# Preparing a head's queries and keys: one GpSimd sum over 128 partitions, rounding on ScalarE, placement by DMA

## The chip, the cores and the metric

The kernel runs on one core of a Trainium2 chip. The metric is the device time of one execution in microseconds, the median of several runs. A core has five engines that run side by side, each with its own stream of instructions in order: TensorE (PE in the profile; PEld are its weight loads), VectorE (DVE), ScalarE (ACT), GpSimd (POOL) and SyncE (SP), which here issues DMAs. They tell each other through semaphores that something is done. SBUF is the memory of 128 partitions from which the engines work; TensorE writes to PSUM.

## The reference

Two decoder layers over 2048 tokens of width 256. The change touches only the second layer's attention, a latent attention with 16 heads:

```python
kv_c = _linear(x, d_kv_w, d_kv_b)               # 2048 x 64
q_c_lat = _linear(x, d_q_w, d_q_b)              # 2048 x 64
q_c = _linear(q_c_lat, u_q_w, u_q_b)            # 16 heads x 128
k_c = _linear(kv_c, u_k_w, u_k_b)
q_r = _rope(_linear(q_c_lat, qr_w, qr_b))       # 16 heads x 64, rotated by position
k_r = _rope(_linear(kv_c, qr_w, qr_b))
scores = einsum('bqhd,bkhd->bhqk', concat(q_c, q_r), concat(k_c, k_r)) * scale
probs = softmax(scores)                         # no mask
ctx = einsum('bhqk,bkhd->bqhd', probs, v)
return _linear(ctx, out_w, out_b)
```

`_rope` makes `x1*cos - x2*sin` and `x1*sin + x2*cos` of every pair of rows.

## The kernel before, in words

The second attention (function `second_attention`) runs over 16 heads x 16 tiles of 128 queries; a tile's number is `n`, its place in the head is 0 to 15 ("tile 12" below is a place). The 2048 keys of a tile are two halves `g` of 1024. float32 precision comes from pairs: a value is rounded to `hi` (type F32R), and `lo` is the rest; products use lo*hi + hi*lo + hi*hi.

For every tile:

- TensorE makes the scores of each half into PSUM (L1078 to L1080, six products), the context of the tile two before (L1094, L1095, 32 products), in half of the time an output product (L1110, five), and one of the next head's preparation products into `psP` (`project`, L1055 to L1062). In its stream the order for a tile is: scores(n + 1, 0), both context halves of n - 2, the output, `project`, scores(n + 1, 1).
- VectorE takes each half's minimum (L1159) and makes the shift (L1167); `low` (L1175) makes the second float16 part of the probabilities, `prob - parts`; both inputs lie in SBUF. In between: `rden` (L1185), and for the next head `rotate` (L1143) or `rest` (L1149).
- ScalarE takes the exponential of each half (L1224), rounds it to float16 (`high`, L1234), takes the context out of PSUM (`both_sums`, L1243), in the next head's preparation `fold` (L1214), and takes outputs (`part`, L1251). `low` needs `high`.
- SP issues a DMA transpose of each half's two float16 parts (L1349), 128 x 2048 x 2 bytes, after `low`; the context products need it landed. In every second head it also transposes a batch of four contexts of half that size (L1359), once in four tiles.
- GpSimd splits contexts (`split`: L1307, L1309, L1311), adds outputs to `x2` (`add`, L1318), and prepares the next head.

Outputs are taken nine tiles late, so they fall on tiles 9 to 15 of the odd heads and 0 to 8 of the even ones behind them.

The next head is prepared in four chunks of 512 tokens, each of three pieces: two products that VectorE multiplies by cosine and sine into `rot[0]` and `rot[1]` (tiles 3j and 3j + 1 for chunk j), and a third whose results `fold` and `rest` take (tile 3j + 2). The sum `rot[0] + rot[1]` has the rotated queries in rows 64 to 127 (`rotary`) and the rotated keys in rows 0 to 63 (`latent`). The queries belong in rows 64 to 127 of `q_hi` and `q_lo`, the keys in rows 64 to 127 of `k_hi` and `k_lo`. Before, GpSimd does it in six instructions of 64 rows x 512, called `join`: the sum rounded into place (`hi`), the same sum unrounded (`whole`), and `whole - hi` (`lo`), first for the queries and then for the keys. Two steps stand in each of the tiles 2 to 13, one ahead of `add` and one behind the wait for `low(n, 0)`, ahead of `split`. After tile 13 `take_weights` copies a head's weights in eight small casts (L1274) and one copy (L1277).

For head 0 the same steps run ahead of the first scores, one after another.

## Time and profile before

| | us |
|---|---|
| median of 3 runs | 2907.39 |
| lowest, highest | 2907.08, 2911.09 |
| the profiled execution | 2912.68 |
| its span, first to last instruction | 2911.4 |
| mean granted TensorE clock in it | 0.921 |

Busy time of the engines over the span: TensorE 2305.6 us (79%), VectorE 2364.0 (81%), ScalarE 1820.9 (63%), GpSimd 1454.5 (50%). A busy share is a mean over stages with different limits, so the rows further down are cut by stage: a row of windows gives the busy time of each engine in a stretch, the granted clock of TensorE (1.00 is 2.4 GHz, 0.50 is 1.2 GHz), the busy share of the DMA engines and the rate. A row of the timeline has the start, the length, the engine, the line, the operation, output <- inputs with their shapes, and in brackets the idle time in front of the instruction and who ended it. The second attention's heads run from 1134 us to 2692 us of the span.

### The profile page before, as it was taken

The page shows a single profiled execution, that of the slowest core. Times are in us where ns is not written, and L with a number is a line of the kernel's source. Part 1 is how long each engine was busy: PE and PEld are TensorE (multiplying, and loading weights), DVE is VectorE, ACT ScalarE, POOL GpSimd, SP SyncE. Part 2 cuts the span into 40 slices and gives each one's busy share as a digit, 9 for nine tenths or more (in the row PEclk, how much of TensorE's full clock was granted, in tenths as well). Part 3 has the DMA queues.
Part 4 walks back from the last instruction along what each step waited for, and adds up shares of the span by engine and source line. Part 5 has one row for each costly group of instructions (what it writes and reads, how often), then busy time and mean ns, then how long its engine had stood idle before and what let it go on. Part 6 is the DMA issues. An engine that isn't in the chain of part 4 may idle for free. (4 is left out here: it accounts for less than half of the span.)

```text
span 2911.4 us, 50632 instructions
## 1 busy us (share of the span) xinstructions
PE 2305.6 (79%) x18576; PEld 1581.4 (54%) x18576; DVE 2364.0 (81%) x3182; ACT 1820.9 (63%) x2455; POOL 1454.5 (50%) x1640
## 2 busy tenths in 40 slices
PE   3688888765665246899888988988888889888699
PEld 1244454422222124667666666776666667666387
DVE  4688888678888465999999999999999999998422
ACT  2677777534333204878777878877777778777211
POOL 2412121036665206677668577676775686752300
PEclk8799999877787567999999999999999999999799
DMA  3000000000000404999999999999999999999200
GB/s 109 1 1 2 1 2 1 1 1 1 1 0 1 98 0 68 184 182 176 181 173 170 189 179 172 186 173 180 175 171 182 175 173 187 175 174 190 68 15 15
DMA packets 1117159, 300.68 MB, mean 103 GB/s; under 512 B 1107121, under 2 KB 1114257, under 8 KB 1116049
## 3 DMA queue, kind: packets, MB, share of 16 engines
q1 hardware_dynamic: 1115104, 295.74, 57.0%
q8 instruction: 149, 2.44, 0.3%
q10 hardware_dynamic: 1808, 1.71, 0.2%
q14 instruction: 98, 0.79, 0.1%
HBM read 18.45 MB, written 2.10 MB: 7 GB/s over the span
## 5 line engine op out<-in xcount | busy, mean ns | idle before, releaser
L1175 DVE TENSOR_TENSOR parts<-prob,parts 128x1024 f16<-128x1024 f32 x512 | 721.0, 1408 | 22.8 <-ACT parts L1234 20.9
L1224 ACT ACTIVATE prob<-psS,shift 128x1024 f32<-128x1024 f32 x512 | 569.7, 1113 | 237.7 <-DVE shift L1167 236.9
L1159 DVE TENSOR_REDUCE lows<-psS 128x1 f32<-128x1024 f32 x512 | 621.0, 1213 | 43.4 <-PE psS L1080 41.3
L1234 ACT CAST parts<-prob 128x1024 f16<-128x1024 f32 x512 | 535.7, 1046 | 15.8
L1094 PE MATMUL psOb<-kv,partsT 128*128 128x130 f16 x4096 | 418.0, 223 | 157.4 <-ACT part L1251 68.5
L1094 PEld LDWEIGHTS psOb<-kv,partsT 128*128 128x128 f16 x4096 | 363.9, 98 | 262.3 <-issue 176.5
L1078 PE MATMUL psS<-k_hi,q_lo 128*128 128x512 f32 x1024 | 432.5, 422 | 37.7 <-ACT prob L1224 29.6
L1095 PE MATMUL psOb<-kv,partsT 128*128 128x66 f16 x4096 | 406.0, 194 | 0.0
L1080 PE MATMUL psS<-k_hi,q_hi 128*128 128x512 f32 x1024 | 404.2, 395 | 0.0
L1079 PE MATMUL psS<-k_lo,q_hi 128*128 128x512 f32 x1024 | 403.8, 394 | 0.0
L1095 PEld LDWEIGHTS psOb<-kv,partsT 128*128 128x128 f16 x4096 | 365.3, 98 | 0.0
L502 ACT ACTIVATE PT<-psS 128x1024 bf16<-128x1024 f32 (+1 forms) x320 | 280.2, 899 | 65.5 <-PE psS L358 40.5
L1078 PEld LDWEIGHTS psS<-k_hi,q_lo 128*128 128x128 f32 x1024 | 194.8, 190 | 147.5 <-ACT prob L1224 90.5
L1307 POOL TENSOR_TENSOR both_sums<-both_sums 128x64 f32<-128x64 f32 x256 | 154.9, 605 | 219.9 <-DVE parts L1175 195.2
L419 DVE TENSOR_REDUCE pm<-psT 128x1 f32<-128x512 f32 (+3 forms) x320 | 207.0, 647 | 51.6 <-PE psT L329 40.2
L751 POOL TENSOR_TENSOR sel<-Lg,two 128x2048 bf16<-128x2048 f32 x32 | 145.2, 4537 | 194.6 <-DVE gap L657 193.3
L550 POOL TENSOR_TENSOR qB<-nmT,blocks 32x512 bf16<-32x512 bf16 x64 | 73.9, 1155 | 306.7 <-DVE qB L435 303.9
L1080 PEld LDWEIGHTS psS<-k_hi,q_hi 128*128 128x128 f32 x1024 | 194.1, 190 | 45.1
L718 ACT ACTIVATE sel<-sel 128x512 bf16<-128x512 bf16 x128 | 78.6, 615 | 214.6 <-DVE sel L664 214.6
L1079 PEld LDWEIGHTS psS<-k_lo,q_hi 128*128 128x128 f32 x1024 | 195.1, 191 | 32.4
L419 DVE TENSOR_REDUCE pm<-psU 128x1 f32<-128x512 f32 (+3 forms) x320 | 181.2, 566 | 22.9 <-PE psU L332 11.1
L355 PE MATMUL psS<-qB,kT 128*128 128x512 bf16 (+3 forms) x640 | 177.8, 349 | 20.5 <-ACT b L479 16.9
(254 smaller groups left out, 4340.6 us busy)
## 6 DMA issues: line engine op xcount, KB each, us to landing
partsT<-parts SPq DMA_TRANSPOSE x512, 4.5
rf<-in_rwT SPq DMA_DIRECT2D x1, 2048.0 KB, 12.1
ef<-in_ewT SPq DMA_DIRECT2D x1, 2048.0 KB, 17.6
trig<-in_trig SPq DMA_DIRECT2D x2, 1024.0 KB, 10.0
outw_s<-in_outwT SPq DMA_DIRECT2D x1, 2048.0 KB, 17.5
out_x<-ot SPq DMA_DIRECT2D x16, 128.0 KB, 1.7
wug<-in_wupT SPq DMA_DIRECT2D x1, 1024.0 KB, 5.5
wug<-in_wgateT SPq DMA_DIRECT2D x1, 1024.0 KB, 7.6
```

The source lines that it names most:

```text
L355: ins = pe.matmul(bank, kT[:, pair % 2, m * P:(m + 1) * P], qB[:, h, c * BANK + r * P:(c + 1) * BANK], start=True, stop=not diag)
L419: dve.tensor_reduce(pm[:, h, r, j:j + 1], psT[n["max"] % 2][:, 0:w], AX_X, ALU.max).then_inc(max_taken, 1)
L502: act.activation(PT[:, h, first:first + width], psS[:, x * BANK:x * BANK + width], ACT.Exp).then_inc(exp_done, 1)
L1078: pe.matmul(bank, q_lo[:, slot, q], k_hi[b][:, k], start=True, stop=False)
L1079: pe.matmul(bank, q_hi[:, slot, q], k_lo[b][:, k], start=False, stop=False)
L1080: ins = pe.matmul(bank, q_hi[:, slot, q], k_hi[b][:, k], start=False, stop=True)
L1094: pe.matmul(psO[:, 0:KW], partsT[:, s, 0, m, :], kv16[:, block, :], start=(block == 0), stop=False)
L1095: ins = pe.matmul(psO[:, 0:REST], partsT[:, s, 1, m, :], kv16[:, block, 0:REST], start=False, stop=(block == NT - 1))
L1159: dve.tensor_reduce(lows[:, n % 2, g:g + 1], psS[:, (2 * n + g) % 3, :], AX_X, ALU.min).then_inc(half_min, 1)
L1175: dve.tensor_tensor(parts[:, s, 1, :], prob[:, g, :], parts[:, s, 0, :], ALU.subtract).then_inc(low_done, 1)
L1224: act.activation(prob[:, g, :], psS[:, (2 * n + g) % 3, :], ACT.Exp, bias=shift[:, n % 2:n % 2 + 1], scale=-1.0).then_inc(exp_done, 1)
L1234: act.copy(parts[:, s, 0, :], prob[:, g, :]).then_inc(high_done, 1)
```

## The change

The six `join` steps of a chunk are replaced. GpSimd makes one sum over all 128 rows into `whole` (`add_up`). ScalarE rounds it into a new tile `rounded` (`round_sums`), between `exponential(n, 1)` and `high(n, 1)`, in tiles 3, 6, 9 and 12. SP copies the two halves of `rounded` into `q_hi` and `k_hi` by two DMAs (`move_sums`), between the transposes of the same tiles. GpSimd makes the two rests (`rest_queries`, `rest_keys`). All three GpSimd steps stand behind the wait for `low(n, 0)`, one a tile in tiles 2 to 13. `rot` has one buffer instead of two. `take_weights` moves from the end of tile 13 to tile 14, behind that tile's `add`. GpSimd's wait for `low_done` 2n now stands in every tile. The first scores of a head wait for rests and moves instead of `joined`.

```diff
-        rot = [sb(L, f"rot{r}", [P, 2, BANK]) for r in range(2)]
-        whole = sb(L, "whole", [C, BANK])
+        rot = [sb(L, f"rot{r}", [P, BANK]) for r in range(2)]
+        whole = sb(L, "whole", [P, BANK])
+        rounded = sb(L, "rounded", [P, BANK], F32R)
...
-                    pe.wait_ge(joined, 24 * (head + 1))
+                    pe.wait_ge(rests_done, 8 * (head + 1))
+                    pe.wait_ge(moved, 128 * (head + 1))
...
-                if 4 * head + j >= 2:
-                    dve.wait_ge(joined, 24 * head + 6 * (j - 1))
+                if 4 * head + j:
+                    dve.wait_ge(added_up, 4 * head + j)
...
+            def round_sums(head, j):
+                c = 4 * head + j
+                act.wait_ge(added_up, c + 1)
+                if c:
+                    act.wait_ge(rests_done, 2 * c)
+                    act.wait_ge(moved, 32 * c)
+                act.copy(rounded[:, :], whole[:, :]).then_inc(round_done, 1)
...
                 exponential(n, 1)
                 if n < TILES and piece_at(n) is not None and piece_at(n) % 3 == 2:
                     fold(n // NT + 1, piece_at(n), 2 * (n + 1))
+                if n < TILES and n // NT + 1 < NH and n % NT in (3, 6, 9, 12):
+                    round_sums(n // NT + 1, n % NT // 3 - 1)
                 high(n, 1)
...
+            def add_up(head, j):
+                c = 4 * head + j
+                pool.wait_ge(rotated, 2 * c + 2)
+                if c:
+                    pool.wait_ge(rests_done, 2 * c)
+                pool.tensor_tensor(whole[:, :], rot[0][:, :], rot[1][:, :], ALU.add).then_inc(added_up, 1)
+                pool.wait_ge(added_up, c + 1)
+
+            def rest_queries(head, j, halves_scored):
+                slot = q_slot(head, j)
+                pool.wait_ge(round_done, 4 * head + j + 1)
+                if halves_scored:
+                    pool.wait_ge(score_ready, halves_scored)
+                pool.tensor_tensor(q_lo[rotary, slot, :], whole[rotary, :], rounded[rotary, :].bitcast(F32),
+                                   ALU.subtract).then_inc(rests_done, 1)
+                pool.wait_ge(rests_done, 8 * head + 2 * j + 1)
...
-                joins = n < TILES and head < NH and 2 <= i <= 13
-                if joins:
+                ahead = n < TILES and head < NH
+                if n < TILES:
                     pool.wait_ge(low_done, 2 * n)
-                    join(head, j, 2 * turn, n)
                 add(n - LATER - 1)
+                if ahead and i == 14 and head + 1 < NH:
+                    take_weights(head + 1)
                 if n < TILES:
                     pool.wait_ge(low_done, 2 * n + 1)
-                if joins:
-                    join(head, j, 2 * turn + 1, n)
+                if ahead and 2 <= i <= 13 and turn == 0:
+                    add_up(head, j)
+                if ahead and 2 <= i <= 13 and turn == 1:
+                    rest_queries(head, j, 2 * (n + 1))
+                if ahead and 2 <= i <= 13 and turn == 2:
+                    rest_keys(head, j)
                 split(n - 3)
-                if n < TILES and i == 13 and head + 1 < NH:
-                    take_weights(head + 1)
...
+            def move_sums(head, j, halves_scored):
+                sp.wait_ge(round_done, 4 * head + j + 1)
+                if halves_scored:
+                    sp.wait_ge(score_ready, halves_scored)
+                sp.dma_start(q_hi[rotary, q_slot(head, j), :].bitcast(F32), rounded[rotary, :].bitcast(F32)).then_inc(moved, 16)
+                sp.dma_start(k_hi[head % 2][rotary, j * BANK:(j + 1) * BANK].bitcast(F32),
+                             rounded[latent, :].bitcast(F32)).then_inc(moved, 16)
...
                     turn_probabilities(n, 0)
+                if n < TILES and n // NT + 1 < NH and n % NT in (3, 6, 9, 12):
+                    move_sums(n // NT + 1, n % NT // 3 - 1, 2 * (n + 1))
                 turn_contexts(n - 4)
```

## Rows read from the trace of the kernel before

**Rows 1.** The page: busy time, share, instructions; and the group of reductions.

```profile
PE 2305.6 (79%) x18576; PEld 1581.4 (54%) x18576; DVE 2364.0 (81%) x3182; ACT 1820.9 (63%) x2455; POOL 1454.5 (50%) x1640
...
L1159 DVE TENSOR_REDUCE lows<-psS 128x1 f32<-128x1024 f32 x512 | 621.0, 1213 | 43.4 <-PE psS L1080 41.3
```

**Rows 2.** Windows by head, `low` (L1175) alone: heads 0, 12, 15, sum.

```profile
1134.30:1226.30 92.00, 42.80 (x32) 1.00 1.01 175
...
2308.30:2405.10 96.80, 46.79 (x33) 1.00 1.02 176
...
2600.90:2692.40 91.50, 39.21 (x32) 0.94 1.11 186
sum 1558.10, DVE 720.97; mean DVE 45.06
```

**Rows 3.** Windows, all engines: heads 1, 12, 13, 15; PE, PEld, DVE, ACT, POOL.

```profile
1226.30:1323.60 97.30, 87.75 (x788) 68.78 (x786) 93.46 (x110) 77.95 (x92) 66.29 (x88) 0.98 1.06 183
...
2308.30:2405.10 96.80, 85.86 (x780) 65.88 (x778) 94.92 (x110) 78.54 (x94) 73.20 (x90) 1.00 1.02 176
2405.10:2503.80 98.70, 87.95 (x787) 68.53 (x784) 92.70 (x109) 77.37 (x92) 65.52 (x88) 0.98 1.04 181
...
2600.90:2692.40 91.50, 74.90 (x708) 59.33 (x705) 76.10 (x92) 71.79 (x85) 21.74 (x55) 0.94 1.11 186
```

**Rows 4.** Timeline of GpSimd and VectorE, one tile of head 12; VectorE in head 13.

```profile
2351.71 1.29 POOL L1291 TENSOR_TENSOR whole<-rot 64x512 f32<-64x512 f32 x1
2353.08 1.60 POOL L1318 TENSOR_TENSOR x<-x,part 128x256 f32<-128x256 f32 x1
...
2351.89 2.20 DVE L1175 TENSOR_TENSOR parts<-prob,parts 128x1024 f16<-128x1024 f32 x1
...
2486.35 1.65 DVE L1175 TENSOR_TENSOR parts<-prob,parts 128x1024 f16<-128x1024 f32 x1
```

**Rows 5.** Timeline at head 13's end: GpSimd, ScalarE, VectorE; windows of the stretch behind.

```profile
2488.93 1.43 POOL L1274 CAST wr_hi<-qr_hi 64x64 fp32r<-64x64 f32 x2
...
2493.57 0.72 POOL L1318 TENSOR_TENSOR x<-x,part 128x256 f32<-128x256 f32 x1
...
2494.38 0.37 ACT L1251 COPY part<-psOb 128x256 f32<-128x256 f32 x1 [3.35 <-POOL x L1318]
...
2496.88 1.23 DVE L1175 TENSOR_TENSOR parts<-prob,parts 128x1024 f16<-128x1024 f32 x1 [2.90 <-ACT parts L1234]
...
2495.00:2498.40 3.40, 3.40 (x38) 3.13 (x36) 1.23 (x1) 3.34 (x4) 1.20 (x3) 0.50 0.63 117
```

**Rows 6.** DMA issues, KB each, median us to landing; windows in the last head.

```profile
partsT<-parts SPq DMA_TRANSPOSE x512, 4.5
rf<-in_rwT SPq DMA_DIRECT2D x1, 2048.0 KB, 12.1
...
out_x<-ot SPq DMA_DIRECT2D x16, 128.0 KB, 1.7
...
2632.00:2648.00 16.00, 14.24 (x136) 11.15 (x136) 15.53 (x19) 13.76 (x17) 2.86 (x10) 1.00 1.17 203
```

**Rows 7.** Groups of ScalarE with shapes: busy us, mean ns, idle before.

```profile
L1224 ACT ACTIVATE prob<-psS,shift 128x1024 f32<-128x1024 f32 x512 | 569.7, 1113 | 237.7 <-DVE shift L1167 236.9
L1234 ACT CAST parts<-prob 128x1024 f16<-128x1024 f32 x512 | 535.7, 1046 | 15.8
...
L1243 ACT ACTIVATE both_sums<-psOb,rden 128x128 f32<-128x128 f32 x256 | 93.7, 366 | 55.4 <-DVE rden L1185 53.7
L718 ACT ACTIVATE sel<-sel 128x512 bf16<-128x512 bf16 x128 | 78.6, 615 | 214.6 <-DVE sel L664 214.6
```

**Rows 8.** Timeline of TensorE in head 13: context products behind a landing, next scores.

```profile
2468.15 0.23 PE L1094 MATMUL psOb<-kv,partsT 128*128 128x130 f16 x1 [0.37 <-DMA partsT<-parts]
...
2470.38 0.50 PE L1078 MATMUL psS<-k_hi,q_lo 128*128 128x512 f32 x1
```

**Rows 9.** Timeline of GpSimd: the last `join` in front of head 0.

```profile
1124.31 1.25 POOL L1294 TENSOR_TENSOR k_lo<-whole,k_hi 64x512 fp32r<-64x512 f32 x1
```

More of the change, by code:

```diff
@@ L1140, in rotate @@
                 dve.wait_ge(piece_ready, 12 * head + piece + 1)
-                if 4 * head + j >= 2:
-                    dve.wait_ge(joined, 24 * head + 6 * (j - 1))
-                dve.scalar_tensor_tensor(out=rot[kind][:, j % 2, :], in0=psP[:, :], scalar=br[kind][:, head:head + 1],
+                if 4 * head + j:
+                    dve.wait_ge(added_up, 4 * head + j)
+                dve.scalar_tensor_tensor(out=rot[kind][:, :], in0=psP[:, :], scalar=br[kind][:, head:head + 1],
                                          in1=trig[:, kind, cols], op0=ALU.add, op1=ALU.mult).then_inc(rotated, 1)
@@ L1254, in scalar @@
                 fold(0, piece, 0)
+                round_sums(0, piece // 3)
             for n in range(TILES + LATER):
@@ L1278, in take_weights, with rest_keys @@
                 pool.wait_ge(weights_in, done + 1)
-            def join(head, j, step, n):
-                cols, b, slot = slice(j * BANK, (j + 1) * BANK), head % 2, q_slot(head, j)
-                done = 24 * head + 6 * j + step
-                if head:
-                    pool.wait_ge(score_ready, 2 * (n + 1))
-                if step == 0:
-                    pool.wait_ge(rotated, 8 * head + 2 * j + 2)
-                rows, hi, lo = ((rotary, q_hi[rotary, slot, :], q_lo[rotary, slot, :]),
-                                (latent, k_hi[b][rotary, cols], k_lo[b][rotary, cols]))[step // 3]
-                if step % 3 < 2:
-                    pool.tensor_tensor((hi, whole[:, :])[step % 3], rot[0][rows, j % 2, :], rot[1][rows, j % 2, :],
-                                       ALU.add).then_inc(joined, 1)
-                else:
-                    pool.tensor_tensor(lo, whole[:, :], hi.bitcast(F32), ALU.subtract).then_inc(joined, 1)
-                pool.wait_ge(joined, done + 1)
+            def add_up(head, j):
[13 more added lines that the diff above has]
+                pool.wait_ge(rests_done, 8 * head + 2 * j + 1)
+            def rest_keys(head, j):
+                pool.wait_ge(round_done, 4 * head + j + 1)
+                pool.tensor_tensor(k_lo[head % 2][rotary, j * BANK:(j + 1) * BANK], whole[latent, :],
+                                   rounded[latent, :].bitcast(F32), ALU.subtract).then_inc(rests_done, 1)
+                pool.wait_ge(rests_done, 8 * head + 2 * j + 2)
             def split(n):
@@ L1323, in gpsimd @@
             for j in range(NB):
-                for step in range(6):
-                    join(0, j, step, None)
+                add_up(0, j)
+                rest_queries(0, j, 0)
+                rest_keys(0, j)
             take_weights(1)
@@ L1360, in turn_contexts @@
                                        ctxp[:, i:i + BATCH, :, :].rearrange("p t a c -> p (t a c)")).then_inc(ctx_landed[b % 2], 16)
+            for j in range(NB):
+                move_sums(0, j, 0)
             for n in range(TILES + 4):
```

3 lines of the change are left out of this document (2 added, 1 removed).

## Prediction, as it was written before the changed kernel had run

> **What bounds the kernel now.** I read the busy shares of the page first: VectorE 81%, TensorE 79%, ScalarE 63%, GpSimd 50% [rows 1]. GpSimd looks harmless, and averages hide where it hurts. So I cut the second attention into its 16 heads, each from its first `low` (L1175, VectorE, the subtraction that makes the second half of the probabilities) to the next head's. The changed code runs in the heads before the last one, as preparation of the next head; the last head has none of it. Heads 0 to 14 take 2600.9 - 1134.3 = 1466.6 us, 97.8 us each; the edges are in the window rows [rows 2]. In head 12 VectorE is busy for 94.9 of 96.8 us [rows 3]: it is the bound there. In the last head it is busy for 76.1 of 91.5 us: with no preparation something else sets the pace.
>
> Second I looked at one VectorE instruction alone, because a bound engine can still run slower than it must. The 32 `low`s of the last head take 39.2 us (1.22 us each), those of head 12 take 46.8 us; all 16 heads sum to 721.0 us [rows 2]. At the last head's length the sum would be 16 x 39.2 = 627.4, so 93.6 us of VectorE time is `low` being longer than its own work. (Some windows count a 33rd instruction at an edge, with almost no time in it.) The timeline says when: a GpSimd sum of 1.29 us starts at 2351.71, the `low` starts at 2351.89 and takes 2.20 us, and GpSimd's next instruction, begun behind that sum, takes 1.60 us [rows 4] where the same form takes 0.72 us elsewhere [rows 5]. So a `low`, whose inputs both lie in SBUF, and a GpSimd instruction hold each other up, and the later one carries the wait.
>
> Third, the odd heads. VectorE idles for 97.3 - 93.5 = 3.8 us in head 1, 6.0 us in head 13, and 45.5 us over the seven odd heads 1 to 13, against 1.9 us in an even head [rows 3]: 45.5 - 7 x 1.9 = 32 us too many. The timeline of head 13's end shows the chain: GpSimd has been copying the next head's weights, so its `add` (L1318) starts only at 2493.57; ScalarE waits 3.35 us for it with `part`; VectorE then waits 2.90 us; and the granted clock of TensorE, which had nothing to do, stands at 0.50 (1.2 GHz) in the 3.4 us behind it [rows 5].
>
> Fourth, the DMA queue: share 1.00 in head 12 [rows 3]. A transpose moves 128 x 2048 x 2 bytes = 0.524 MB. The best rate over 16 us that I found is 203 GB/s [rows 6], so 2.58 us a transpose if that is the queue's limit.
>
> **The change part by part.**
>
> *Sums and rests on GpSimd.* A chunk has six instructions of 64 rows x 512 now; it gets three: one sum over 128 rows and two rests. The 128-row sum isn't in the trace. A 64x512 form takes 1.25 to 1.29 us [rows 4, 9] and a 128x256 form 0.72 us [rows 5]: time goes by columns, not rows, so 1.27 us for the sum too. Between 1.27 and 2.54 us (if 128 rows cost twice) I take 1.27. GpSimd loses 12 x 1.27 = 15 us a head. That is off the path; what counts is where the rest falls. Today each of 12 tiles has one join before `low(n, 0)` and one after it. Now all three stand after the wait for `low(n, 0)`, beside VectorE's rotation and reduction, which read PSUM. The collision of rows 4 is gone in ten of the twelve tiles. What is left: tile 12 has a rest but no rotation, and a `low` that meets such an instruction there takes 1.65 us today [rows 4], 0.43 too many; tile 13's adds may meet a `low` for 0.4 to 1.0 us; in tiles 3, 6 and 9 the rest waits for ScalarE and pushes the context split into a `low`, for about 0.1 us each. That makes 1.7 us a head, 26 us in all, of 93.6. **Saved: 68 us.**
>
> *Take_weights behind `add`.* At tile 14 the `add` now runs first, then the weights; the next `add` is due a tile later. The weights took 4.6 us (2488.93 to the add at 2493.57 [rows 5]), against a tile of over 5 us, so ScalarE no longer waits. Of the 32 us some 6 lie at heads' starts, where I see other causes. **Saved: 26 us**; if the late weights only move the wait one tile on, nothing.
>
> *Rounding on ScalarE.* 128x512 from SBUF takes 0.62 us (L718) [rows 7], and 4 a head. ScalarE's tile is 2 x 1.113 + 2 x 1.046 [rows 7] + 0.37 for `both_sums` + 0.37 for `part` [rows 5, 7] = 5.06, with a round 5.68, with seven pipeline gaps of 0.03 about 5.9. VectorE's work without collisions is (94.9 - 7.6) / 16 = 5.5 us a tile on average [rows 2, 3]; in tile 12, where it neither rotates nor rests, two reductions of 1.21 [rows 1], two `low`s of 1.22 and under 0.4 of small ones leave about 5.1. So tiles 3, 6 and 9 lose 0.3 us where an output is taken too (three a pair of heads), and tile 12 loses 0.4 to 0.8 us, in part beside the collision there. Queued behind the round are `high(n, 1)` and through it `low(n, 1)`. **Cost: 12 us**; between 0 (hidden) and 4 x 0.62 x 15 = 37 (all on the path).
>
> *Moves by DMA.* Two a chunk, 64 rows x 2 KB = 131 KB each, 8 a head, on SP's queue between two transposes, so the second transpose of that tile and the TensorE products on it stand behind them. A move inside SBUF isn't in the trace. From below: 2048 KB landed in 12.1 us, 128 KB of that is 0.76 us; from above: 128 KB of output landed in 1.7 us, start and end included [rows 6]. The queue takes 0.76 us more nearly, since transfers overlap in it: median 4.5 us from issue to landing with 2.6 us of work [rows 6]. The wait of SP for the round hides: `turn(n, 1)` needs `high(n, 1)`, which is behind the round anyway. A head's queue work is then 32 x 2.58 + 2.6 (context transposes, four of half size in every second head) + 8 x 0.76 = 91.3 us. The engines' account gives (1466.6 - 68 - 26 + 12) / 15 = 92.3 us a head. So the queue comes within 1%, transposes will land late at times, and TensorE's order puts the next scores behind them: from the context products' start at 2468.15 to the scores' at 2470.38 are 2.2 us of products queued behind one landing [rows 8]. **Cost: 8 us**; from 0 to 60 (4 us a head, a quarter of the idle time that the last head shows).
>
> The Trainium skill has another figure, page "DMA: Bandwidth & Descriptors", section "Latency and other measured facts": 261 GB/s for a DMA transpose with a non-contiguous middle dimension. By that a transpose is 2.0 us, an estimate, and the queue would be no bound at all. No stretch of this trace shows more than 203.
>
> *First head.* The six joins of the last chunk, 1.27 us and 0.07 between them, took 8.0 us in front of the first scores; the row is the sixth [rows 9]. Now sum, fold and round, then moves and rests side by side: 1.3 + 1.3 + 2.7 = 5.3 us, with waits nearer 6. **Saved: 2 us.** VectorE's single buffer `rot` costs nothing: `add_up` is done two tiles ahead of the next rotation.
>
> Sum: -68 - 26 + 12 + 8 - 2 = -76 us. The profiled execution took 2912.7 (span 2911.4), the median of the runs is 2907.4; 5.3 lower. 2912.7 - 76 - 5.3 = **2831 us**.
>
> **The rivals.**
>
> *A, the queue is no bound* (12%): transposes keep up, rounds hide mostly. For it: 203 GB/s was seen, not shown to be a ceiling. Against: VectorE idles 15 us in the last head, with GpSimd nearly empty. Collisions all but gone (-88), stall gone (-32), rounds +2, first head -2: 2907 - 120 = 2787 us.
>
> *B, collisions move* (18%): rests and splits, late behind the round, meet `low(n, 1)`. GpSimd instructions: 12 joins a head at 0.4 us = 72 us, so of 93.6 only 22 are saved; stall -26; ACT +4 as it is then hidden: -44 or 2863 us. Late landings that bring the clock to 0.50, as in the stretch of rows 5, end near the same: 60 instead of 8 us gives 2883.
>
> *C, slower by the queue* (7%): a move holds the queue for its whole 1.7 us. Then a head is 32 x 2.58 + 2.6 + 8 x 1.7 = 98.8 us against 97.8: +15 us, 2922 us. It decides from (97.8 - 85.2) / 8 = 1.6 us a move. Against: the 2048 KB row. The skill's same page, section "Anatomy of one DMA", gives about 2 us fixed plus bytes at 436 GB/s (for the GpSimd path): as an estimate 2.3 us a move; it says that most of it is completion latency, not occupancy.
>
> *D, no change* (3%): gains of VectorE come back one for one as waits for landings. 2907 us.
>
> **How the numbers follow.** Forecast 60%: 2831, its own range 2810 to 2855. Within 8 in 10: from 2785, at A, to 2880, over B. Outside are C and D, a tenth, and as much again for the tails of the others. This kernel's measurement tells about 0.2%, 6 us, from no change. Faster 0.90 (forecast, A, B), same 0.04 (D and a part of C), slower 0.06.
>
> **What would show it.** Right: `low` in heads 0 to 14 near 1.22 to 1.28 us mean; ScalarE's wait for `x` at the odd heads' ends gone, and the stretches at clock 0.50 with it; VectorE busy under 95% of a head; DMA rate near 200 GB/s; heads of 91 to 94 us. Wrong: `low(n, 1)` longer than now (B); moves that land in over 2 us of extra queue time and SP's issues late throughout (C); heads near 88 us with DMA at over 205 GB/s (A). The forecast fails most easily in the 8 us for late landings, which no tile of this trace tests at this load.

## The result, and the profile after

The changed kernel takes 2926.14 us (median of 5 runs, 2923.19 to 2931.91) against 2907.08 on the same chip: ratio 1.0067, 95% interval 1.0050 to 1.0084. It is slower, by 19 us, where I had forecast 76 us less. The profiled execution took 2931.91 us, with a span of 2930.6.

One correction of what stands ahead: the rotated queries lie in rows 0 to 63 of the sum and the keys in rows 64 to 127, and both go to rows 0 to 63 of `q_hi` and `k_hi`; I had the row numbers the wrong way round. No number hangs on it.

The page of after: busy times, two groups of VectorE, and three DMA issues (KB each, median us to landing).

```profile
PE 2315.4 (79%) x18576; PEld 1597.3 (55%) x18576; DVE 2283.6 (78%) x3182; ACT 1835.6 (63%) x2519; POOL 1085.3 (37%) x1448
...
L1162 DVE TENSOR_REDUCE lows<-psS 128x1 f32<-128x1024 f32 x512 | 623.2, 1217 | 142.8 <-PE psS L1083 140.2
L1178 DVE TENSOR_TENSOR parts<-prob,parts 128x1024 f16<-128x1024 f32 x512 | 632.0, 1234 | 4.6 <-ACT parts L1245 2.7
...
partsT<-parts SPq DMA_TRANSPOSE x512, 4.7
q_hi<-rounded SPq DMA_DIRECT2D x64, 128.0 KB, 3.4
k_hi<-rounded SPq DMA_DIRECT2D x64, 128.0 KB, 2.9
```

The windows of after by head: head 12, 13 and 15 with all engines (PE, PEld, DVE, ACT, POOL, granted clock, DMA share, GB/s), then head 12 and the sum for `low` alone.

```profile
2321.00:2423.20 102.20, 88.94 (x786) 69.19 (x784) 88.17 (x110) 78.98 (x98) 47.02 (x78) 0.97 1.03 179
2423.20:2524.40 101.20, 88.00 (x782) 68.85 (x781) 88.73 (x108) 78.49 (x96) 44.32 (x76) 0.97 1.06 188
...
2622.60:2711.40 88.80, 71.45 (x703) 56.37 (x701) 76.35 (x93) 71.68 (x85) 18.89 (x55) 0.98 1.13 190
...
2321.00:2423.20 102.20, 39.15 (x33) 0.97 1.03 179
...
sum 1579.60, DVE 631.93; mean DVE 39.50
```

What the change was to do, it did. GpSimd's busy time fell from 1454.5 [rows 1] to 1085.3 us, and `low` (now L1178) from 720.97 [rows 2] to 631.93 us: the collisions are gone. But head 12 takes 102.2 us where it took 96.8 [rows 3], with VectorE busy for 88.2 of them and not for 94.9. VectorE has 6.8 us less to do in this head and waits 12.1 us more. The first reductions (`lows`, a half's minimum) show for what: their idle time grew from 43.4 [rows 1] to 142.8 us over the whole run, nearly all of it for scores (`psS`). The gain of VectorE came back as waits for TensorE.

And TensorE waits for transposes. The timeline of after in tiles 3 to 5 of head 12; tile 5 is the longest of that head (start, duration, engine, line):

```profile
2343.87 1.21 SPq L1380 DMA_DIRECT2D q_hi<-rounded  x1
2344.06 1.21 DVE L1178 TENSOR_TENSOR parts<-prob,parts 128x1024 f16<-128x1024 f32 x1
2345.13 0.59 SPq L1381 DMA_DIRECT2D k_hi<-rounded  x1
2345.82 1.31 SPq L1391 DMA_TRANSPOSE ctxT<-ctxp  x1
...
2347.22 18.04 SPq L1373 DMA_TRANSPOSE partsT<-parts  x5
...
2351.99 1.23 DVE L1178 TENSOR_TENSOR parts<-prob,parts 128x1024 f16<-128x1024 f32 x1
2353.37 0.23 PE L1097 MATMUL psOb<-kv,partsT 128*128 128x130 f16 x1 [3.37 <-DMA partsT<-parts]
...
2355.57 0.17 DVE L1188 RECIPROCAL rden<-psOb 128x1 f32<-128x1 f32 x1 [2.35 <-PE psOb L1113]
...
2356.98 0.79 PE L1081 MATMUL psS<-k_hi,q_lo 128*128 128x512 f32 x1
```

The same stretch as windows, with the granted clock and the DMA rate last:

```profile
2349.90:2353.30 3.40, 0.10 (x3) 0.00 (x0) 3.32 (x3) 3.04 (x3) 1.85 (x2) 1.00 1.21 121
2353.30:2356.90 3.60, 3.53 (x24) 2.27 (x24) 0.17 (x1) 0.00 (x0) 2.13 (x4) 0.59 1.11 249
2356.90:2361.80 4.90, 4.90 (x18) 3.69 (x18) 1.78 (x3) 2.70 (x5) 0.00 (x0) 0.61 0.55 103
```

To be read from the top: the two moves and a transpose of contexts stand between the tile's two transposes in SP's order. The `low` that the second transpose follows ended by 2345.3; the transpose is issued at 2347.22, 1.9 us late, since SP issues the three others first, and it goes into a queue that has these three to serve. (That the issuing by itself isn't the cause, the version with the moves on ScalarE's queue shows below.) TensorE runs dry at 2350.0 and waits 3.37 us for a landing. It comes back at a granted clock of 0.59, against 1.00 before, near the lower of its two levels (1.2 GHz), so the twelve score products from 2356.98 take 4.75 us, until 2361.73. VectorE, whose part of tile 5 began at 2351.99, starts the next tile's at 2364.64: 12.65 us for one tile.

### The profile page after: what moved, and what is told of

Read it like the earlier page. It is cut to its first block and busy times, and to the rows that moved or that the text cites. A ratio compares the mean times of both kernels' runs of the same rounds, so it can differ in the third digit from the quotient of the medians.

```text
span 2930.6 us, 50703 instructions
## 1 busy us (share of the span) xinstructions
PE 2315.4 (79%) x18576; PEld 1597.3 (55%) x18576; DVE 2283.6 (78%) x3182; ACT 1835.6 (63%) x2519; POOL 1085.3 (37%) x1448
## 5 line engine op out<-in xcount | busy, mean ns | idle before, releaser
L1162 DVE TENSOR_REDUCE lows<-psS 128x1 f32<-128x1024 f32 x512 | 623.2, 1217 | 142.8 <-PE psS L1083 140.2
L1178 DVE TENSOR_TENSOR parts<-prob,parts 128x1024 f16<-128x1024 f32 x512 | 632.0, 1234 | 4.6 <-ACT parts L1245 2.7
L1097 PE MATMUL psOb<-kv,partsT 128*128 128x130 f16 x4096 | 423.9, 222 | 188.2 <-DMA partsT<-parts 170.3
L1082 PE MATMUL psS<-k_lo,q_hi 128*128 128x512 f32 x1024 | 410.7, 401 | 0.0
L1083 PE MATMUL psS<-k_hi,q_hi 128*128 128x512 f32 x1024 | 410.2, 401 | 0.0
L1327 POOL TENSOR_TENSOR both_sums<-both_sums 128x64 f32<-128x64 f32 x256 | 105.4, 412 | 204.3 <-DVE parts L1178 183.9
```

What stands on the lines that cost most here:

```text
L1082: pe.matmul(bank, q_hi[:, slot, q], k_lo[b][:, k], start=False, stop=False)
L1083: ins = pe.matmul(bank, q_hi[:, slot, q], k_hi[b][:, k], start=False, stop=True)
L1097: pe.matmul(psO[:, 0:KW], partsT[:, s, 0, m, :], kv16[:, block, :], start=(block == 0), stop=False)
L1162: dve.tensor_reduce(lows[:, n % 2, g:g + 1], psS[:, (2 * n + g) % 3, :], AX_X, ALU.min).then_inc(half_min, 1)
L1178: dve.tensor_tensor(parts[:, s, 1, :], prob[:, g, :], parts[:, s, 0, :], ALU.subtract).then_inc(low_done, 1)
```

## The experiments

Each expectation names its theories; a letter holds within the texts of one group. A tile's time is from its first `low` to the next tile's, as a mean over the even heads 2 to 14 or the odd heads 1 to 13.

**First group: which part takes the gain back.** Four edits. One lets GpSimd put the rounded halves in place with copies of 64x512, two a chunk, instead of the moves:

```diff
+                if ahead and 4 <= i <= 14 and i % 3 != 0:
+                    place(head, (i - 4) // 3, int(i % 3 == 2), 2 * (n + 1))
                 add(n - LATER - 1)
...
-                if n < TILES and n // NT + 1 < NH and n % NT in (3, 6, 9, 12):
-                    move_sums(n // NT + 1, n % NT // 3 - 1, 2 * (n + 1))
```

> The changed kernel with GpSimd copies (64x512, one input, about 0.6 us each) in the place of the DMA moves; they stand ahead of the add, beside VectorE's first reduction. Theory M (the moves on SP's queue delay the transposes behind them, TensorE waits for landings and its clock falls): VectorE keeps its gain, 2830 to 2850 us. Theory S (the queue is full with the transposes alone, so a faster VectorE can only wait): 2890 to 2910 us, waits for landings as in the changed kernel.

2843.83 us, ratio 0.9779 (0.9763 to 0.9794), as theory M had it. It leaves nothing out, and is faster than both kernels.

One is the kernel before, with only `take_weights` behind tile 14's `add` (and GpSimd's wait for `low(n, 0)` in that tile, which the other tiles have):

```diff
+                if n < TILES and i == 14:
+                    pool.wait_ge(low_done, 2 * n)
                 add(n - LATER - 1)
+                if n < TILES and i == 14 and head + 1 < NH:
+                    take_weights(head + 1)
...
-                if n < TILES and i == 13 and head + 1 < NH:
-                    take_weights(head + 1)
```

> The kernel before with take_weights alone moved behind tile 14's add. The prediction's term says -26 us, 2881 us, with ScalarE's wait for x at the odd heads' ends gone. Rival: the stretch at clock 0.50 and the idle time come back from late landings, no change, 2900 to 2910 us.

2895.76 us, ratio 0.9951 (0.9935 to 0.9968): 12 us, where my sum had 26.

One leaves the moves out (the rounded rotated halves never reach the scores):

```diff
-                if n < TILES and n // NT + 1 < NH and n % NT in (3, 6, 9, 12):
-                    move_sums(n // NT + 1, n % NT // 3 - 1, 2 * (n + 1))
```

> The changed kernel with the move DMAs left out: the rotary rows of q_hi and k_hi stay zero, so that part of the scores is missing; everything else runs as in the changed kernel. Theory M: 2825 to 2845 us, VectorE's idle time over heads 0 to 14 falls from about 150 us to 50. Theory S: over 2890 us.

2842.86 us, ratio 0.9770 (0.9755 to 0.9784). The group of the first reductions in it, and of `low`:

```profile
L1182 DVE TENSOR_TENSOR parts<-prob,parts 128x1024 f16<-128x1024 f32 x512 | 633.3, 1237 | 5.1 <-ACT parts L1248 3.2
L1166 DVE TENSOR_REDUCE lows<-psS 128x1 f32<-128x1024 f32 x512 | 623.4, 1218 | 68.6 <-PE psS L1082 65.4
```

`low` is as short as after, and the wait for scores is 68.6 us and not 142.8. So sums, rounds, rests and weights on their own bring 64 us, and the moves cost 83 us: 60 pairs at 1.38 us. In the trace VectorE's idle time shows it in two places, not corrected for overlap: 74 us more of this wait, and 16 us more ahead of `rden`. Theory M holds. TensorE's wait for the moves themselves is no part of it: after, that is one wait of 4.4 us, in front of head 0.

And one issues the moves from GpSimd's queue:

```diff
+                pool.dma_start(q_hi[rotary, slot, :].bitcast(F32), rounded[rotary, :].bitcast(F32)).then_inc(moved, 16)
+                pool.dma_start(k_hi[head % 2][rotary, j * BANK:(j + 1) * BANK].bitcast(F32),
+                               rounded[latent, :].bitcast(F32)).then_inc(moved, 16)
```

> The changed kernel with the same two moves a chunk issued from GpSimd's queue instead of SP's. If it is SP's time and its order (a move takes 1.5 us of issuing a chunk, and the next transpose stands behind it) that costs: 2840 to 2860 us. If it is the work that the moves put on the DMA engines: 2915 to 2930 us, as the changed kernel.

2963.51 us, ratio 1.0180 (1.0163 to 1.0197). Its row of `low`:

```profile
L1178 DVE TENSOR_TENSOR parts<-prob,parts 128x1024 f16<-128x1024 f32 x512 | 697.4, 1362 | 5.1 <-ACT parts L1245 3.0
```

SP's sequencer is free of the moves, and the time is outside both ranges: worse. But this edit changes two things. The waits stay, and the collisions are back (697.4 against 632.0 us), and the timeline says how, here in head 6:

```profile
1800.52 0.53 POOL L1307 DMA_DIRECT2D q_hi<-rounded  x1 [2.06 <-DVE parts L1178]
1801.05 0.52 POOL L1308 DMA_DIRECT2D k_hi<-rounded  x1
1801.58 1.28 POOL L1310 TENSOR_TENSOR q_lo<-whole,rounded 64x512 fp32r<-64x512 f32 x1
1801.99 1.96 DVE L1178 TENSOR_TENSOR parts<-prob,parts 128x1024 f16<-128x1024 f32 x1
```

The two issues take 1.05 us of GpSimd's stream, so its rest starts late and meets the next `low`, which takes 1.96 us and not 1.23. 57 of the 60 rests behind moves overlap a `low` of over 1.35 us, and these 57 hold 53 of the 65 us. So this run doesn't separate SP's issuing from the queue's work; the one on ScalarE's queue below does.

**Second group: what of a move costs.** Its bytes, its queue, or its place. Half the columns in each move (the other half of the rounded rotated queries and keys is left out):

```diff
+                h = BANK // 2
+                sp.dma_start(q_hi[rotary, q_slot(head, j), 0:h].bitcast(F32), rounded[rotary, 0:h].bitcast(F32)).then_inc(moved, 16)
+                sp.dma_start(k_hi[head % 2][rotary, j * BANK:j * BANK + h].bitcast(F32),
+                             rounded[latent, 0:h].bitcast(F32)).then_inc(moved, 16)
```

> The changed kernel with as many moves, each of 256 instead of 512 columns (the other half of the rounded columns stays zero, so that part of the scores is missing). The runs so far: without moves 2843, with them 2926, 0.69 us for each of 120 moves. Theory Q (the moves' work on the DMA engines, 0.6 us each by their packets, comes on top of transposes that fill them): half of it goes, 2875 to 2895 us. Rival N (what costs is a DMA as such, its issue, its start, its completion): 2915 to 2930 us.

2915.50 us, ratio 1.0025 (1.0014 to 1.0036), in rival N's range. Half the bytes take off some 11 of 83 us. In the packet records of heads 0 to 14 no transpose's packet starts for 1.21 us (mean) around a pair of whole moves, and for 1.10 us around a pair of half ones. The Trainium skill, page "DMA: Bandwidth & Descriptors", section "Rules for kernel authors", says that below 64 KB a transfer is mostly overhead; here the pair costs the queue nearly the same at 128 KB a move, too.

One move at a time, in the tiles 4, 5, 7, 8, 10, 11, 13 and 14:

```diff
+                if n < TILES and n // NT + 1 < NH and 4 <= n % NT <= 14 and n % 16 % 3 != 0:
+                    move_sums(n // NT + 1, (n % NT - 4) // 3, 2 * (n + 1), (n % NT % 3 - 1,))
```

> The changed kernel with the queries' move one tile later and the keys' move two tiles later, so that no two moves stand together, and none with the context transpose in tile 3 of the even heads. Theory Q: the same work, 2915 to 2930 us. Rival P (the place costs: two moves and a context transpose ahead of one transpose make one long wait and a clock of 0.50): even heads come down from 102 to 97 us, 2880 to 2895 us in all.

2975.11 us, ratio 1.0223 (1.0208 to 1.0238), the slowest of all, yet tiles 0 to 11 take 72.5 us in both kinds of heads (even heads after: 79.5) and tile 5 of even heads 7.25 (11.05). The loss is in one place, which TensorE's row names:

```profile
L1081 PE MATMUL psS<-k_hi,q_lo 128*128 128x512 f32 x1024 | 434.0, 424 | 110.4 <-DMA k_hi<-rounded 103.6 <-ACT prob L1235 6.2
```

The keys of the last chunk are moved in tile 14, and the next head's first scores wait for them, about 6.6 us a head. Place, not bytes, is the lead.

From ScalarE's queue, at the end of its tile:

```diff
+                if n < TILES and n // NT + 1 < NH and n % NT in (3, 6, 9, 12):
+                    move_sums(n // NT + 1, n % NT // 3 - 1, 2 * (n + 1))
```

> The changed kernel with the same moves issued by ScalarE at the end of its tile, so SP issues transposes only. Theory Q: the engines have the same work, 2915 to 2930 us. Rival I (SP's issuing, 1.6 us a chunk, and the order in its one queue cost): 2850 to 2875 us.

2945.53 us, ratio 1.0125 (1.0105 to 1.0144), outside both ranges, and 19 us more than with SP's queue. `low` stays at 631.1 us, so there are no new collisions, SP issues transposes only, and still tile 5 of even heads takes 9.79 us. What costs is not that SP issues the moves. It is the moves' share of the DMA engines or their place, which the next runs take apart.

And the kernel before with 120 such moves into rows that nothing reads:

```diff
+                if n < TILES and n // NT + 1 < NH and n % NT in (3, 6, 9, 12):
+                    sp.wait_ge(score_ready, 2 * (n + 1))
...
+                    sp.dma_start(whole_wide[latent, :], trig[rotary, 0, 0:BANK]).then_inc(moved, 16)
```

> The kernel before with the moves alone added: 8 a head of the same size, between the same transposes, from the table of cosines to rows that nobody uses. VectorE is slow here, so the transposes have slack. Theory Q: a head's queue work goes from 85.2 to 90.4 us; the heads without changes went at no more than 0.915 of queue work by time, so 98.8 us instead of 97.8: 2920 to 2935 us. If VectorE's slack covers them: 2905 to 2912. If every move costs its 0.69 us here too: 2990.

2943.05 us, ratio 1.0113 (1.0084 to 1.0142), between the expectation's first range and its last. Here no engine needs what a move brings, and nothing was gained that could be given back, and 60 pairs still cost 35 us, 0.58 each. Against 1.38 after: the same moves cost less in a kernel whose VectorE is late anyway.

**Third group: which places, and what bounds the rest.** The spread version mended (none after tile 13):

```diff
+                places = {4: (0, 0), 5: (0, 1), 7: (1, 0), 8: (1, 1), 10: (2, 0), 11: (2, 1), 12: (3, 0), 13: (3, 1)}
```

> The changed kernel, with one move at a time: of each chunk's sum the queries' half is moved in one tile and the keys' half in the next (tiles 4,5, 7,8, 10,11 and 12,13), none in a tile that also moves a context, and none after tile 13, so that the next head's first scores don't wait. Theory P (place): two moves issued together beside a context's transpose delay one transpose past what TensorE has in hand, and a single move does not. Tiles 0 to 11 take what they took in the first run with spread moves (72.5 us in both kinds of heads), tiles 12 to 15 about 22 to 24 as after, so heads 0 to 14 about 15 x 95 = 1425 to 1445 us and the kernel 2855 to 2880 us. Theory N (each move costs its 0.7 us wherever it stands, 120 of them 83 us): 2915 us or more, and no tile is free of it.

2888.01 us, ratio 0.9925 (0.9907 to 0.9942): 38 us of the 83 are back; 8 us short of what the theory of the place had said, and 27 below the other's. Both moves together, one tile later:

```diff
-                if n < TILES and n // NT + 1 < NH and n % NT in (3, 6, 9, 12):
+                if n < TILES and n // NT + 1 < NH and n % NT in (4, 7, 10, 12):
```

> The changed kernel, with both moves of a chunk still issued together, but one tile later (tiles 4, 7, 10, 12), so not in the tile that also moves a context through the queue. If the pair by itself is what the queue's slack can't take, the time stays at 2910 to 2930 us and the long tile comes one tile later. If it is the pair together with the context's transpose, the long tile goes, and the time falls to 2865 to 2890 us. By the theory that each move costs the same wherever it stands it stays at 2920 or more.

2890.40 us, ratio 0.9938 (0.9918 to 0.9958), at the edge of what the coincidence with the context's transpose had said, and the same as with single moves: that two moves go together is not what costs. Tiles 3 and 4 and then tile 5 of head 12, in this version:

```profile
2315.69:2326.86 11.17, 10.27 (x101) 8.03 (x99) 11.10 (x16) 8.96 (x14) 7.57 (x10) 1.00 1.19 195
2326.86:2334.04 7.18, 6.60 (x56) 5.17 (x57) 5.86 (x8) 6.49 (x9) 2.91 (x5) 1.00 0.99 201
```

and after:

```profile
2340.82:2351.99 11.17, 8.79 (x78) 6.74 (x76) 11.10 (x15) 8.95 (x14) 7.56 (x10) 1.00 1.23 201
2351.99:2364.64 12.65, 11.27 (x78) 8.59 (x79) 5.96 (x8) 6.49 (x9) 2.87 (x5) 0.73 0.55 114
```

VectorE has the same work in both, to 0.1 us; the long tile and its clock of 0.73 are gone.

Third, the version with GpSimd's copies, with only the upper parts transposed (the low half of the probabilities is left out):

```diff
-                sp.dma_start_transpose(partsT[:, s, :, :, :].rearrange("p a m q -> p (a m) q"),
-                                       parts[:, s, :, :].rearrange("p a k -> p (a k)")).then_inc(landed[s], 16)
+                sp.dma_start_transpose(partsT[:, s, 0, :, :], parts[:, s, 0, :]).then_inc(landed[s], 16)
```

> The version in which GpSimd's copies take the place of the moves, with the lower half of each transpose left out (only the high parts are transposed, the low part is zero), which leaves out the rests of the scores' weights: it measures the queue, which then carries half as much. The version with whole transposes took 2843.8 us. If landings of transposes still end tiles there (the queue's rate sets the heads), the time falls by 3 us a head and more, to 2800 us or below. If TensorE and VectorE set them, it stays within 10 us of 2843.

2795.84 us, ratio 0.9611 (0.9597 to 0.9625). (The expectation names the part badly: it is the low half of the probabilities that is left out, nothing of the scores.) VectorE's wait for scores over heads 1 to 14, in the list of waits (us, times, longest), here

```profile
DVE lows L1164 <- PE psS L1083: 5.6, 14, 0.6
```

and with whole transposes:

```profile
DVE lows L1162 <- PE psS L1083: 38.0, 63, 1.6
```

So landings still cost 48 us in the best version, without any move. The two profiled executions differ by 54.8 us: 3.0 us a head in heads 0 to 14 (1411.3 to 1366.6, 44.7 in all) and 10 in the last head.

**Fourth group: the 47 us between later pairs and copies.** The single moves of the first three chunks, and copies by GpSimd for the last:

```diff
                     rest_keys(head, j)
+                if ahead and i in (13, 14):
+                    place(head, int(i == 14), 2 * (n + 1))
                 split(n - 3)
```

> The version with single moves (2888.0 us, 45 us above the one without moves), with the last chunk's two moves of each head replaced by GpSimd copies in tiles 13 and 14; the six moves of the first three chunks stay in tiles 4, 5, 7, 8, 10, 11. Theory L (the slack): tiles 12 to 15 have 4.92 us of VectorE's work and two transposes that take the queue 2 x 2.58 = 5.16 us, so a move there has nothing to hide in, while tiles 0 to 11 (5.5 to 5.9 us) have room for one. The time falls by 15 x 2.5 us to 2845 to 2858 us, and tiles 12 to 15 take the 20.3 to 21.8 us that they take without moves. Theory N (each move costs the same wherever it stands): 30 of 120 moves are gone, a quarter of 45 us: 2877 us.

2940.08 us, ratio 1.0110 (1.0093 to 1.0127): neither theory. The timeline at the end of head 12 shows an error of mine:

```profile
2422.44 1.63 POOL L1293 CAST wr_lo<-qr_lo 64x64 fp32r<-64x64 f32 x2
...
2424.13 0.18 POOL L1296 COPY beta_h<-beta 64x1 f32<-64x1 f32 x1
2424.38 0.61 POOL L1326 CAST k_hi<-rounded 64x512 fp32r<-64x512 f32 x1
...
2425.25 0.76 PE L1083 MATMUL psS<-k_hi,q_lo 128*128 128x512 f32 x1 [4.63 <-POOL k_hi L1326]
...
2428.18 1.22 DVE L1164 TENSOR_REDUCE lows<-psS 128x1 f32<-128x1024 f32 x1 [4.50 <-PE psS L1085]
```

I had put the keys' copy at the end of GpSimd's tile 14, behind the nine copies of weights, and the next head's first scores wait for it. A copy of 0.61 us, in the wrong place, holds up this head's end by 4.5 us. The theory of the slack was not tested by it; two more versions do that, with the copies ahead of `add`. One keeps pairs of moves at tiles 4, 7 and 10 and copies the last chunk:

```diff
+                if ahead and 4 <= i <= 14 and i % 3 != 0 and (i - 4) // 3 in (3,):
+                    place(head, (i - 4) // 3, int(i % 3 == 2), 2 * (n + 1))
...
-                if n < TILES and n // NT + 1 < NH and n % NT in (4, 7, 10, 12):
+                if n < TILES and n // NT + 1 < NH and n % NT in (4, 7, 10):
```

> The version with both moves of a chunk together at tiles 4, 7, 10, 12 (2890.4 us, 46.6 us above the one with GpSimd's copies, 2843.8), with the last chunk's two moves of heads 1 to 15 replaced by GpSimd's copies, in tiles 13 and 14 and this time ahead of GpSimd's addition to the output, as in the version with copies alone. Theory L (the slack): tiles 12 to 15 have 4.92 us of VectorE's work and two transposes that take the queue 2 x 2.58 = 5.16 us, so a pair of moves there has nothing to hide in; tiles 0 to 11 with 5.5 to 5.9 us have room. Then the last chunk's moves carry most of the 46.6 us, and the time is 2848 to 2862 us. Theory N (a pair costs the same in every place): a quarter of 46.6 us goes, 2879 us.

2868.64 us, ratio 0.9870 (0.9854 to 0.9887). The other is its complement:

```diff
+                if ahead and 4 <= i <= 14 and i % 3 != 0 and (i - 4) // 3 in (0, 1, 2):
...
-                if n < TILES and n // NT + 1 < NH and n % NT in (4, 7, 10, 12):
+                if n < TILES and n // NT + 1 < NH and n % NT == 12:
```

> The complement: GpSimd's copies for the first three chunks (tiles 4 to 11), and only the last chunk's pair of moves through the queue, at tile 12. Theory L: nearly all of the 46.6 us stays, 2874 to 2888 us. Theory N: a quarter of it stays, 2855 us. If the two versions' costs over 2843.8 don't add up to about 46.6 us, the moves act on each other across tiles (a queue that has not caught up from one pair when the next comes).

2868.75 us, ratio 0.9872 (0.9855 to 0.9890). Both theories are half right. Over the version with copies (2843.8) the costs are 24.8 and 24.9 us, which add up to 49.7 where both together cost 46.6. The 3 us between them are within the noise of these ratios (some 5 us each), so no effect of the pairs on each other is to be seen. The 15 pairs at tile 12 cost 1.66 us each, more than their 1.2 us in the queue; the 45 at tiles 4, 7, 10 cost 0.55. In tile 12 VectorE's tile takes 4.92 us without moves, and two transposes are 5.16 us of queue at 203 GB/s; that a pair there costs the full amount fits, and that one in a tile of 5.58 or more costs a third of it. The loss shows two tiles on: tile 14 of even heads takes 8.02 us with the pair at tile 12 and 5.33 with copies alone.

Last, the coincidence. A context's transpose is issued in tile 3 of even heads and in tiles 7, 11 and 15 of odd ones. I had overlooked the odd heads when I wrote the expectation of the later pairs, and the trace had it: with a pair at tile 7, tile 9 of odd heads took 8.37 us (6.21 without moves), two tiles behind the coincidence, like tile 5 of even heads after. Taking that pair to tile 8:

```diff
-                if n < TILES and n // NT + 1 < NH and n % NT in (4, 7, 10, 12):
+                if n < TILES and n // NT + 1 < NH and n % NT in (4, 8, 10, 12):
```

> The version with pairs of moves at tiles 4, 7, 10, 12 (2890.4 us), with the second pair at tile 8. I had overlooked there that odd heads transpose a context in tiles 7, 11 and 15 (even heads in tile 3), so its pair of tile 7 stands beside one, and two tiles later, in tile 9 of odd heads, a tile takes 8.37 us instead of 6.2. Theory K (a pair of moves and a context's transpose in one tile): tile 9 of odd heads falls to about 6.5 us, 7 x 2 = 14 us: 2872 to 2882 us. If the coincidence is no cause, 2886 to 2894 us, with the long tile at 10 or gone without gain.

2889.21 us, ratio 0.9933 (0.9918 to 0.9947). No gain in the total, which is the range of the theory that the coincidence is no cause. Tile 9 fell to 7.17, not to 6.5; and a new wait came, 29.2 us in 15 places:

```profile
DVE lows L1162 <- PE psS L1083: 90.7, 98, 2.6
...
ACT rounded L1226 <- DMA k_hi<-rounded: 29.2, 15, 3.1
```

ScalarE's next round, in tile 9, writes the one buffer `rounded` that the pair of tile 8 still reads. Whether this wait took the gain back, no run shows; for tile 7 of odd heads the price of the coincidence stays open. And the changed kernel with nothing but the coinciding pair shifted:

```diff
-                if n < TILES and n // NT + 1 < NH and n % NT in (3, 6, 9, 12):
+                if n < TILES and n // NT + 1 < NH and n % NT in (3 if n // NT % 2 else 4, 6, 9, 12):
```

> The changed kernel (2926.1 us) with a single pair of moves shifted, that of the first chunk, from tile 3 to tile 4, in even heads alone, where tile 3 also transposes a context. Theory K: tile 5 of even heads, 11.05 us after and 7.34 without moves, falls to about 7.4 us, in 7 or 8 heads: 26 to 30 us, 2896 to 2902 us. If any pair costs what its place among short and long tiles gives, a shift of 8 pairs of 60 by one tile changes less than 5 us: 2921 or more.

2902.31 us (10 runs, 2892.99 to 2911.03), ratio 0.9978 (0.9964 to 0.9991). Eight of sixty pairs, one tile later, are worth 24 us; seven of them stood beside a context's transpose (in head 0 there is none): 3.4 each. Tile 5 of even heads fell from 11.05 to 7.34 us, what it is without moves (7.34); 7 x 3.71 = 26 us. This shows what taking the pair out of tile 3 is worth. How much of it is the coincidence and how much the tile, two other rows say. In odd heads, where tile 3 has no context's transpose, a pair there lengthens tile 5 from 6.10 (no moves) to 7.03 us after, by 0.9. And in the kernel before, with moves added at tile 3, tile 5 grows from 6.93 to 9.10 in even heads and from 6.24 to 6.52 in odd ones. So most of it, some 2 to 3 us a time, goes with the context's transpose, and up to 0.9 with the place.

| version | us | tile 5, even heads | tile 9, odd heads | tiles 12 to 15, even, odd |
|---|---|---|---|---|
| after | 2926.1 | 11.05 | 6.62 | 23.0, 23.1 |
| first pair at 4 in even heads | 2902.3 | 7.34 | 6.30 | 23.8, 23.1 |
| pairs at 4, 7, 10, 12 | 2890.4 | 7.39 | 8.37 | 24.0, 23.6 |
| pairs at 4, 8, 10, 12 | 2889.2 | 7.33 | 7.17 | 23.8, 23.8 |
| last chunk copied | 2868.6 | 7.43 | 7.67 | 20.8, 22.0 |
| last chunk moved alone | 2868.8 | 7.18 | 6.10 | 23.5, 23.6 |
| all copied | 2843.8 | 7.00 | 6.69 | 20.8, 22.2 |
| no moves | 2842.9 | 7.34 | 6.21 | 20.2, 21.1 |

## Why the prediction was wrong, step by step

**What bounds the kernel: right, but not whole.** VectorE, lengthened by collisions, was the bound of heads 0 to 14, and the sum went by that. The version without moves has heads 0 to 14 of 1397.1 us, 93.1 each, where the engines' account had 92.3. But the halved transposes show that the queue was a second bound right behind, also without a move.

**Collisions: right, and larger.** 68 us forecast; `low` fell by 89 us (720.97 to 631.93). The sum over 128 rows takes 1.29 us and the one over 64 took 1.28, so the rows cost nothing, as assumed.

**`take_weights`: right mechanism, half the size.** 26 us forecast, 12 measured. With that edit alone ScalarE's wait for `x` shrank from 29.6 to 11.0 us (after, where no join stands ahead of `add`, it is gone). The odd heads fell by 4.4 us each, 31 in all, and the even ones rose by 2.1, 1.7 of it in tile 1. That rise is landings again: TensorE's waits for them in tiles 0 and 1 of even heads went from 0.8 to 1.9 us a head, and between the two versions with GpSimd's copies tile 1 takes 7.28 us with whole transposes and 5.59 with halved ones. The gain was sized about right; half of it came back from the queue.

**Rounds: too dear.** 12 us forecast. Without moves, tiles 3 and 6 with a round last 5.58 us, as tiles 4 and 7 without one do, and tile 12 lasts 4.92. Tile 9 of odd heads, which takes an output too, lasts 6.21, but 5.58 with halved transposes, round and output and all. So the rounds are hidden, as far as tile lengths show; no run took them out.

**Not all of it arrives.** By these the version without moves should be some 100 us faster; it is 64. Collisions took 88 us off `low` there (721.0 to 633.3), and 25 of them came back in one row, the first reductions' idle time, 43.4 [rows 1] to 68.6 us. That is rival D in small, and the halved transposes say where it comes from. The other 13 us have no place in this account; the profiled executions of the two kernels lie 69 us apart and not 64, which makes up 5 of them.

**Moves: the step that failed.** "Cost: 8 us; from 0 to 60." It is 83 us. A move's own work was not the error: 0.76 us forecast, and a pair leaves a gap of 1.21 us. I compared the queue's work with the engines' over a whole head, 91.3 to 92.3 us, and concluded that it fits. It has to fit tile by tile. Two transposes are 4.8 to 5.2 us (at 217 or 203 GB/s) of a tile of 5.58, so a tile leaves 0.4 to 0.8 us, and tile 12, of 4.92, next to none; a pair with a context's transpose behind it puts in 1.2 and about 1.3 us at once, and what is late then is paid by TensorE two tiles on, before the queue has caught up. Where the wait is long, as the 3.37 us shown, it is paid twice, since TensorE returns near half its clock: in heads 1 to 14 after, its granted clock stands at the lower level in 16 stretches, 75 us together, and in one of 3.4 us without moves. After, TensorE is busy for 1226.7 us there with the work that takes 1195.4 without moves. The bounds failed with it: 60 us was a guess from the last head's idle time and no reckoning of a single tile.

By place: 24 us more for the pairs of tile 3 in even heads, beside a context's transpose, than a tile later (measured by the shift), 25 us for the pairs at tile 12 (measured by the complement, so in a version without the other pairs), and the rest, some 34 us, for the 45 pairs outside tile 12, 0.75 each, without a cause shown beyond their time in the queue.

**Rivals.** C came nearest, 2922 us, by luck, for a reason that the runs refute: it had moves that hold the queue for 1.7 us each, where a pair leaves a gap of 1.21, and heads as long as the queue's work. That most of a move's time isn't occupancy, as C's paragraph says, these rows bear out: the moves land in 3.4 and 2.9 us (median). Even heads after (2 to 14) move 174 to 185 GB/s and odd ones 188 to 195, so the long heads are those in which the queue is least used. B's second half, late landings with the clock near 0.50, is what happened, from a base of fewer collisions; its first half did not: `low` is 1.23 us.

A was right in one point, and the prediction's sentence that no stretch of the trace shows more than 203 GB/s was wrong: two windows of 16 us show 210 before and 217 after.

```profile
1222.78:1238.78 16.00, 14.14 (x137) 11.15 (x136) 15.57 (x19) 12.85 (x15) 3.89 (x10) 1.00 1.18 210
...
2275.78:2291.78 16.00, 14.06 (x145) 11.38 (x144) 15.03 (x19) 12.51 (x18) 7.89 (x14) 1.00 1.15 217
```

At 217 a transpose is 2.4 us and not 2.58, and the queue's work in a head some 86 us and not 91: the average left more room than I had thought, and the moves still cost 83 us. But A's conclusion fails, since the queue is a bound. By the Trainium skill's 261 GB/s (page "DMA: Bandwidth & Descriptors", section "Latency and other measured facts") the 32 transposes of a head take 64 us of its 93, an estimate, and halved transposes would have changed little; they took 48 us off. A stretch of 3.6 us above shows 249, right behind one of 3.4 us with 121; both together are 187.

**First head: right.** The first `low` starts at 1131.8 instead of 1134.3: 2.5 us for 2 forecast; in the other runs with the changed start it lies between 1129.8 and 1133.5, and in two more with the old one at 1133.6 and 1133.7.

Of the places where the forecast would break I had named the right one, "the 8 us for late landings", and given it a tenth of its size.

## What to carry to other kernels

Work added to a nearly full queue is to be weighed against the slack of the tile that it lands in, together with whatever else that tile issues, and not against the average over a head: the same pair of moves cost 0.55 us in one group of tiles, 1.66 in another, and 3.4 more in the one tile where it stood beside another transfer. When a change frees the engine that sets the pace, first ask what the next one is late by; here 89 us were freed on `low`, and the queue, next in line, took more than that back with the moves' help. A small copy on a half-idle engine was the better carrier for 128 KB (two of 0.61 us against a pair of moves of 1.2 us on the full queue), as long as it isn't queued behind something that the next head doesn't need yet.

## What the runs showed of the hardware

A plain move between two transposes costs the queue about the same for 64 KB as for 128 KB: 1.10 and 1.21 us without a new transpose packet, for a pair. Single moves leave 0.65 us each.

GpSimd's copies of 64x512 take 0.61 us, its sums of the same shape 1.28. With the copies `low` sums to 653.9 us, without them to 633.3. Of the 77 `low`s over 1.35 us, 28 meet a copy, and 60 meet an `add`, which stands behind the copy and starts later for it. The Trainium skill, page "SBUF — State Buffer", section "SBUF: two separate sides", tells of a port pair that VectorE with two SBUF inputs and a GpSimd instruction that reads SBUF hold exclusively, one after the other. The 20 us agree, and so do the 697.4 us when GpSimd issues the moves, where a rest meets the `low`.

```profile
L1178 DVE TENSOR_TENSOR parts<-prob,parts 128x1024 f16<-128x1024 f32 x512 | 653.9, 1277 | 6.8 <-ACT parts L1245 5.0
```

Also without moves the transposes' packets pause. In heads 0 to 14 of the kernel before there are 124 gaps of over 0.6 us between the starts of two of them (mean 0.9), and 57 in the version without moves. Of the 124, 54 lie within 1.5 us of a 16 KB packet of the queue that the profile calls "instruction", where gaps strewn at random would give about 31. No run took that queue's traffic away, so this is a coincidence in time and not a cause shown.
